# Cross attention's first keys and values are made in the self stage, with the output projection, norm and queries in waves of chunks behind it

## What is computed

```python
x = x + gate * (self_attention(norm(x)) @ w_so + b_so)      # keys: the batch's 256 tokens
q = norm(x) * scale + shift @ w_q                           # "cq"
k, v = ctx @ w_k + b_k, ctx @ w_v                           # "ck", "cv", 1601 keys
x = x + gate * (softmax(q k / sqrt(8)) v @ w_co + b)        # layer 2: only the 16 largest scores
x = x + gate * mlp(norm(x))
```

## Time and profile before

| | |
|---|---|
| median of 3 runs | 4952.71 us (4948.7 to 4954.18) |
| profiled execution | 4945.83 us, its span 4944.1 us |
| granted TensorE clock, mean | 0.798 of full |
| busy share | PE 70%, DVE 73%, ACT 58%, POOL 11% |
| six attention stages begin at | 188, 398, 1193, 1406, 2249 and 2476 us |

### The profile page before, as it was taken

How to read it: one execution, slowest core, us unless ns; L and a number is a source line. 1 busy time by engine, 2 the same in 40 slices (tenths; PEclk the granted TensorE clock), 3 DMA queues, 4 the chain that set the end, 5 groups by cost and what they waited for, 6 DMA issues and landing times. The chain is left out here.

```text
span 4944.1 us, 75874 instructions
## 1 busy us (share of the span) xinstructions
PE 3477.9 (70%) x28020; PEld 1517.5 (31%) x28020; DVE 3632.0 (73%) x5577; ACT 2860.3 (58%) x5351; POOL 556.4 (11%) x1277
## 2 busy tenths in 40 slices
PE   2575999975759999865636656565666665578987
PEld 2222333322223333332213223232322222235553
DVE  6555888935567888735479999999999999923223
ACT  1353888853517887834437777777777776622123
POOL 1011212100114334001100100000010100000000
PEclk7776999986769999976657777767776777689999
DMA  4424434204343343115231101110110100001000
GB/s 129 115 53 104 98 88 102 62 20 106 66 102 87 75 94 82 33 49 100 60 68 37 36 23 32 31 38 22 34 39 21 33 13 13 2 21 34 20 0 9
DMA packets 270142, 265.81 MB, mean 54 GB/s; under 512 B 48976, under 2 KB 238808, under 8 KB 269016
## 3 DMA queue, kind: packets, MB, share of 16 engines
q1 hardware_dynamic: 269784, 261.10, 22.1%
HBM read 150.71 MB, written 109.09 MB: 53 GB/s over the span
## 5 line engine op out<-in xcount | busy, mean ns | idle before, releaser
L1096 ACT ACTIVATE prob<-x_ps 128x512 f32<-128x512 f32 (+1 forms) x2880 | 1563.5, 597 | 426.0 <-PE x_ps L994 401.9
L1187 DVE TENSOR_REDUCE mpart<-ring 128x1 f32<-128x400 f32 (+2 forms) x2816 | 1292.7, 523 | 325.2 <-PE ring L942 321.9
L942 PE MATMUL ring<-k_st,q_st 52*128 52x400 bf16 (+2 forms) x3584 | 860.8, 372 | 436.3 <-ACT s_sb L1078 320.4
L1013 PE MATMUL av_ps<-prob,va 128*16 128x256 f32 (+1 forms) x11520 | 990.0, 433 | 2.3 <-ACT o_sb L1102 1.8
L994 PE MATMUL x_ps<-q_st,k_st 55*128 55x256 bf16 x5504 | 625.1, 302 | 78.4 <-ACT prob L1096 48.7
L989 PE MATMUL x_ps<-neg_id,un 128*128 128x128 bf16 (+1 forms) x3328 | 364.1, 276 | 364.0 <-ACT prob L1096 362.4
L1069 ACT ACTIVATE un<-s_sb 128x1601 fp8e4<-128x1601 f32 x256 | 392.7, 1535 | 352.0 <-DVE s_sb L1213 352.0
L942 PEld LDWEIGHTS ring<-k_st,q_st 52*128 52x128 bf16 x3584 | 256.1, 101 | 952.6 <-ACT s_sb L1078 400.4
L1078 ACT ACTIVATE s_sb<-ring 128x400 f32<-128x400 f32 (+1 forms) x1024 | 472.0, 525 | 43.7 <-PE ring L942 35.5
L1202 DVE MAX8 mpart<-s_sb 128x8 f32<-128x1601 f32 x256 | 455.2, 1826 | 20.0 <-ACT s_sb L1078 20.0
L1206 DVE MATCH_REPLACE8 s_sb<-mpart,s_sb 128x1601 f32<-128x1601 f32 x256 | 463.2, 1824 | 0.0
(11 more groups left out here) (194 smaller groups left out, 3294.5 us busy)
## 6 DMA issues: line engine op xcount, KB each, us to landing
k_st<-kc_dram SPq DMA_DIRECT2D x192, 300.2 KB, 5.3
kc_dram<-k SPq DMA_DIRECT2D x432, 100.0 KB, 2.3
q_dram<-pj_q SPq DMA_DIRECT2D x144, 128.0 KB, 2.3
q_st<-q_dram SPq DMA_DIRECT2D x80, 192.0 KB, 3.8
kc_dram<-k SPq DMA_DIRECT2D x144, 100.2 KB, 2.3
ctx_t<-in_ctxT SPq DMA_DIRECT2D x16, 800.5 KB, 5.1
o_dram<-o_sb SPq DMA_DIRECT2D x768, 9.0 KB
k_dram<-pj_q SPq DMA_DIRECT2D x72, 128.0 KB, 2.3
```

The source lines that it names most:

```text
L942: nc.tensor.matmul(ring_ps[:, r % BANKS, 0:w], q_st[rows, b % NQ, 2 * t + pl, qt * P:(qt + 1) * P], k_st[rows, slot_of(n), pl, c0:c0 + w], ...
L1013: last = nc.tensor.matmul(av_ps[32 * k:32 * k + VW, n % 2, :], va[0:sizes[j], b % NVB, j, G * t + k, :], prob[0:sizes[j], s % NPROB, (2 * ...
L1096: nc.scalar.activation(prob[0:size, s % NPROB, hf * 512:(hf + 1) * 512], x_ps[0:size, (2 * s + hf) % XBANKS, :], ACT.Exp, scale=HEAD_SCALE ...
L1187: nc.vector.tensor_reduce(mpart[:, n % 4, row, c:c + 1], ring_ps[:, r % BANKS, 0:chunks[c][1]], AX.X, ALU.max).then_inc(g["red"].sem, 1)
```

## The change

`stage_project(cross)` is gone. What it did is a class `Onward`, called at the end of the self stage; the keys and values of batch 0 are items of the self stage's plan. The order of the waves: chunk c begins at wave FIRST[c], and in each wave every begun chunk does its next step.

```diff
+Q_AHEAD = 2
...
+        self.va = self.sb("va", [P, 2, CT, NH, VW])
...
+            nc.gpsimd.memset(p.va[:], 1.0).then_inc(loaded.sem, 1)
...
+class Onward:
+    FIRST = (0, 1, 2, 5)
+    OP, MEAN, VAR, DIAG, NORM, PROJ = range(6)
...
+    def waves(self, first, upto):
+        for w in range(first, upto):
+            for c in range(NC):
+                k = w - self.FIRST[c]
+                if 0 <= k < 6:
+                    yield k, c
...
+    def pe(self, pe, ready, exps, ocopy):
...
+            if k == self.OP:
+                pe.wait_ge(ready.sem, ready.at(2 * c + 2))
...
+                nc.tensor.matmul(self.bank[:, c, :], weight(p, self.layer, "so"), p.o_all[:, cols], start=True, stop=True).then_inc(s["op"].sem, 1)
...
+            elif k == self.MEAN:
...
+                pe.wait_ge(s["x"].sem, s["x"].at(c + 1))
...
+    def pool(self, pool, table):
+        done = 0
+        for c in (1, 2):
+            done = self.split(pool, self.p.nc.gpsimd, self.s["pchain"], done, c, self.s["pparts"], table)
...
+    def sp(self, sp, x_done, stores):
+        p, s = self.p, self.s
+        k_st = p.k_flat[:].rearrange("p (t h c) -> p t h c", t=NG, h=2)
+        sp.wait_ge(x_done.sem, x_done.at(2 * NU * 2))
+        for st in stores:
+            sp.wait_ge(st.sem, st.at(192))
+        for t in range(NG):
+            for hf in range(2):
+                sp.dma_start(k_st[64 * hf:64 * hf + STACK, t], p.kc_dram[0, 2 * t:2 * t + 2, hf].rearrange("h r c -> r h c")).then_inc(s["loaded"].sem, 16)
+        for c in range(NC):
+            parts = s["dparts" if c in (0, 3) else "pparts"]
+            sp.wait_ge(parts.sem, parts.at(1 + c // 2))
+            for j in range(GROUPS):
+                sp.dma_start(p.q_dram[:, :, j * HD:(j + 1) * HD, c * CH:(c + 1) * CH].rearrange("h f d c -> (h f) d c"), self.q3[:, c, Q_PART[j]]).then_inc(s["st" if c else "st0"].sem, 16)
+            if c == 0:
+                sp.wait_ge(s["st0"].sem, s["st0"].at(16 * GROUPS))
+                for b in range(Q_AHEAD):
+                    for hf in range(2):
+                        sp.dma_start(p.q_st[64 * hf:64 * hf + STACK, b], p.q_dram[:, hf, :, b * T:(b + 1) * T].rearrange("h r c -> r h c")).then_inc(s["loaded"].sem, 16)
...
+            for b in range(1, B) if cross else [0]:
...
+        if not self.cross:
+            return (4 if self.KU == 8 else 8) * (i + 1)
...
+        if not self.cross:
+            return 36 + 4 * i
...
+            load_ctx(B0)
...
-                for b, c in kstore_at[-1]:
-                    store_k(b, c)
-                for n in kload_at[-1]:
-                    load_k(n)
-                load_ctx(1)
...
+            if onward:
+                onward.sp(sp, g["x"], [g["kst0"], g["kst1"]])
...
-                nc.vector.memset(va[:], 1.0).then_inc(g["init"].sem, 1)
...
+                if onward and k == END + 2:
+                    onward.dve_begin(dve)
+                    onward.dve(dve, 0, 2, table)
                 for b in recip_at.get(k, []):
                     recip(b)
+                if onward and k == END + 6:
+                    onward.dve(dve, 2, 3, table)
+            if onward:
+                if rope:
+                    dve.wait_ge(g["tab"].sem, g["tab"].at(16))
+                onward.dve(dve, 3, onward.ALL, table)
```

More of the change, by code:

```diff
@@ L484, in stage_project @@
             table = p.sb("pj_table", [P, 2, T], F32, ctx)
[L485 to L486 removed]
+        va = p.sb("pj_va", [P, NV, 4, NH, VW], F32, ctx)
         pp = p.ps("pj_ps", [P, 3, CH], ctx)
[L488 removed]
         block = ctx.enter_context(nc.Block())
@@ L525, in _ @@
                     nc.tensor.matmul(pp[:, n % 3, :], weight(p, layer, names[r]), norm.h[:, c, :], start=True, stop=True).then_inc(proj.sem, 1)
[L526 to L535, removed]
+            for g in range(NV):
+                m = NI * stepn + g
+                if g < 3:
+                    pe.wait_ge(pf.sem, pf.at(m - 2))
+                else:
+                    pe.wait_ge(v_out.sem, v_out.at(g - 2))
+                for k in range(4):
+                    last = nc.tensor.matmul(pp[:, m % 3, k * P:(k + 1) * P], norm.h[:, g, k * P:(k + 1) * P], weight(p, layer, "v"), start=True, stop=True)
+                last.then_inc(v_mm.sem, 1)
         @block.scalar
@@ L547, in _ @@
                 ins.then_inc(pf.sem, 1)
[L548 to L558, removed]
+            act.wait_ge(ones_r.sem, ones_r.at(1))
+            for g in range(NV):
+                m = NI * stepn + g
+                act.wait_ge(v_mm.sem, v_mm.at(g + 1))
+                nc.scalar.activation(va[:, g, :, :, 0:HD], pp[:, m % 3, :].rearrange("p (k h d) -> p k h d", k=4, d=HD), ACT.Copy).then_inc(v_out.sem, 1)
+        @block.gpsimd
+        def _(pool):
+            nc.gpsimd.memset(va[:], 1.0).then_inc(ones_r.sem, 1)
         @block.vector
         def _(dve):
-            if cross:
-                out.dve(dve)
             norm.dve(dve)
@@ L584, in _ @@
                 done += 3
[L585 to L591, removed]
+    v_mm.passed(NV)
+    v_out.passed(NV)
+    v_st.passed(32 * NV)
+    ones_r.passed(1)
     if rope:
@@ L678, in stage_attention @@
     masked = layer == 2 and not cross
-    rope = layer == 1 and cross
+    rope = layer == 1
     biased = layer != 1
@@ L687, in stage_attention @@
     KSTEP = 2 if rope else 1
-    KU, VU = (4 * KSTEP, 4) if cross else (0, 0)
+    KU, VU = 4 * KSTEP, 4
+    B0 = 1 if cross else 0
+    ahead = range(1, B) if cross else [0]
+    q_index = lambda b: b // NQ + (1 if not cross or b % NQ >= Q_AHEAD else 0)
     BANKS, XBANKS = 4, 3
```

318 lines of the change are left out of this document (227 added, 91 removed).

## The result

The changed kernel took 4841.28 us (median of 3, 4840.75 to 4842.8) against 4952.71: a ratio of 0.9785, 95% interval 0.9772 to 0.9798. The forecast was 4866, a ratio of 0.9825, 25 us too slow; the result lies inside the stated range (4822 to 4908), but 6 us under the forecast's own range (4847 to 4884). The profiled execution took 4842.8 us with a span of 4841.0, so 103.1 us of span against the earlier trace rows.

The account below looks back on a forecast made before the run. No single engine bounds the whole; SP's queue is full in the self stage. 139 - 46 - 2 - 4 = 87 us saved from 4952.7 gives 4866 us, range 4822 to 4908.

Parts of the forecast that it names:

- The waves, 139 us: Last value matmul to cross stage's first score: 139 us saved over three layers, between 121 (low clock) and 158 (high).
- The late normalise: End of self stage: DVE's first waves delay the last normalise by 10 us at low clock, 5.8 at high.
- The prediction's 111: Cross stages' start: batch 0's keys and values no longer made there, first score earlier, 111 us gained over three layers.
- The key stores, 46 us on SP: Self stages: four groups of six key stores on SP's full queue cost 15.4 us per layer, 46 in all.
- absorbed: Rival: SP's key stores in the self stage cost almost nothing; 133 us saved, 4820 us; chance 0.12.
- slower at 1.8 us a store: Rival: SP's key stores issue slowly in the self stage; kernel slower from 1.8 us each, 4978 at 2.16; chance 0.04.
- The engines' part, costed at nothing: Self stages: PE's and ACT's added work for keys and values costs nothing; up to 29 us if not covered.
- The table of layer 1 (2 us): Start of self stage: layer 1's 1.6 MB table load delays the first row loads, 2 us taken between 0 and 10.
- GpSimd beside DVE, 4 us: Waves: two of chunk 3's DVE steps slowed by GpSimd beside them, 0.7 us each, 4 us for three layers.
- The signs of being wrong: Self stage grows under 8 or over 25 us; first score waits beyond zero matmul; GpSimd's chunk 2 ends the stage.
- Waves without use: Rival: waves at the self stage's end hide nothing; 30 us saved, 4923 us; chance 0.12.
- Engines without cover: Rival: new matmuls and copies between scores stall the self stage, all 29 us of PE's added; 4895 us; chance 0.12.

Follow-up runs that it names:

- e12: The changed kernel as it is, measured once more on the same chip as three other runs: ratio 0.9792 to the kernel before.
- e3: The changed kernel with only key tile 0 loaded at the self stage's end, tiles 1 to 3 at the cross stage's start: ratio 0.9793.
- e7: Half the change: batch 0's keys and values in the self stage, projection in its own stage, key loads waited for at that stage's end: ratio 0.9896.
- e9: The changed kernel with one store for each six key stores and twelve key loads of eight rows instead of eight loads: ratio 0.9850.
- e10: The changed kernel with one store for six, twelve eight-row key loads, and half of chunk 3's query stores on ACT's queue: ratio 0.9843.
- e5: The changed kernel with two long-row stores for each six key stores in the self stage, so scores read misplaced keys: ratio 0.9727.
- e1: The changed kernel with each group of six key stores in the self stage issued twice: ratio 0.9893.
- e6: The changed kernel with each self-stage matmul that makes batch 0's keys and values issued twice into the same bank: ratio 0.9805.
- e11: The changed kernel with the four chunks one after another instead of in waves: ratio 0.9958.
- e2: The changed kernel with the self stage's key stores issued by ACT's queue instead of SP's, at the same steps: ratio 0.9763.

## Why the prediction was right, point by point

**The waves, 139 us.** Measured 138.9 (40.5, 51.4 and 47.0 by layer), in e12 140.2. The forecast took the middle between the low clock (121) and the high one (158; its figures by layer add up to 120 and 157); the clock was 0.79 to 0.88 up to the last normalise and 0.61 to 0.67 behind it. That the middle fits so well is partly luck. SP's wait behind the key loads (2.9 us in layer 0, 0.9 in layer 2, against the 6.1 of e3) was not in the layout, and its premise, that the self stage's tail runs at the low clock, held in one layer of three. The late normalise was 6.0, 4.5 and 6.4 us later, near the high clock's 5.8 and not the low one's 10; batch 6's reciprocal came 7.0 us after the last value matmul, not 10. Chunk 3 ends the stage and not GpSimd's chunk 2, ready at 381.8, as forecast. Keys alone are worth 91 of the 139 (e7). The prediction's 111 for them shrinks by 20 where the projection keeps a stage of its own: the query loads then stand ahead of the first score, 3.5 us a layer, and the three layers together take 10 us longer from last value to next stage.

**The key stores, 46 us on SP.** The self stage up to its last row load grew by 51.5 us (mean of seven executions). The four store counts, 12, 24, 72 and 144 for the three layers, give 440.2 (e9, e10), 449.9, 474.8 and 528.6 us. From 12 to 72 a store costs 0.58 us; the line reaches 433 at none, so the stores' part is 42 us, against a forecast of 46. (The stores of e5 and e9 are fewer and larger, but take as long to issue, 0.59 us.) The step was right in mechanism and size, and the rivals "absorbed" and "slower at 1.8 us a store" are both refuted by e1. The time alone would not have told: 4841 lies 25 us from the forecast and 21 from "absorbed" (4820). The experiments separate the two, and what brought the result so near to that rival is the term that the sum missed, below.

**The engines' part, costed at nothing.** This term was most likely too small. At no stores 433 us are left where the kernel before had 423.3: some 10 us for the new matmuls, copies, splits and the context load together, but from a line drawn past its points and against a single profile. e6 points the same way: 25 us of the same matmuls once more cost 6 to 8 us. "SP's queue, always full, is what they can be waiting for" was then too strong: idle time of 25 of 105 us did not make all of it free. Why is not shown; that they sit between scores in the ring is the likely reason, and the copies and GpSimd's splits were never tried alone. The table of layer 1 (2 us) cannot be told from this.

**GpSimd beside DVE, 4 us.** The diagonal on DVE took 0.93 to 1.62 us in four of its twelve instances, each time just behind the start of a GpSimd operation (three times of chunk 2's split, once of the last normalise), instead of 0.63 to 0.69. For chunk 3's, the ones that I had priced, that is 0.6, 0.2 and 0.9 us more in layers 0 to 2; its residual, the other one, never met GpSimd and kept its 0.69. So 1.8 us stand against the 4 forecast, and they are inside the 138.9 measured, where I had counted them on top. Layers 0 and 1 of the changed kernel, both engines in order of time:

```profile
359.45 0.63 DVE L764 TENSOR_TENSOR on_f<-const,on_rstd 128x512 f32<-128x512 f32 x1
359.48 1.18 POOL L1348 TENSOR_TENSOR o_all<-num,rden 128x256 f32<-128x256 f32 x1 [5.37 <-DMA rden<-r_dram]
...
363.50 0.72 POOL L1348 TENSOR_TENSOR o_all<-num,rden 128x256 f32<-128x256 f32 x1 [2.84 <-DMA rden<-r_dram]
363.55 1.22 DVE L764 TENSOR_TENSOR on_f<-const,on_rstd 128x512 f32<-128x512 f32 x1
...
1354.81 1.27 POOL L714 TENSOR_TENSOR on_f<-on_f,table 128x512 f32<-128x512 f32 x1 [15.54 <-ACT on_h L705]
1355.35 0.69 DVE L769 TENSOR_TENSOR on_h<-on_h,xa_ps 128x512 f32<-128x512 f32 x1 [4.59 <-PE xa_ps L668]
...
1360.44 0.61 POOL L724 CAST on_q<-on_f 128x512 bf16<-128x512 f32 x1
1360.67 0.93 DVE L764 TENSOR_TENSOR on_f<-const,on_rstd 128x512 f32<-128x512 f32 x1 [0.27 <-ACT on_rstd L686]
```

The product with its operand in PSUM (`xa_ps`) keeps its 0.69 us beside GpSimd's, the diagonal with both in SBUF does not. All four slow diagonals end 0.55 us after the GpSimd operation that had begun before them, as if they had stood still until it was over; at 359.45 the diagonal began first, kept its 0.63, and GpSimd's product took 1.18 instead of 0.72. The rule of the Trainium skill that the forecast weighed (SBUF — State Buffer, "Who interferes with whom") says the same, and the 20 us of the other reading did not come.

**The sum, 87 us, was 16 us too small** by the first pair of profiles (103.1). The terms above account for little of it: 4 more from the last point, 4 from the stores, 2 from the table, 10 less for the engines, and 4 more because this profile's 470.9 lies that much under the mean. Together that is 4 of the 16. The rest, less 2 us lost elsewhere in the program, is a term I did not have, the stretch from last row load to last value matmul: 43.5 us in all before, 30.0 after, so 13.5. It was left out of the sum, and how large it comes out is a matter of the execution: in e12 it is 5.8, and from self stages to first scores 93.8 us are saved where the forecast says 87. Over the seven executions of the same code the stretches sum to 26 to 40 us, mean 34.5, which is 9 less than in the one profile of before. That the change causes it is not shown: it follows the clock, below. By medians the gain was 111 us in the first measurement. The profile of before lies 6.9 us under its median and that of after 1.5 over, and what no row explains of the 111 is in that.

**The signs of being wrong.** One of them came up. "It is wrong if the self stage grows by under 8 us or over 25 in a layer": up to the last value matmul layer 0 grew by 7.8 us, layers 1 and 2 by 12.6 and 13.6. Up to the last row load, where SP's stores act, it was 15.2, 16.5 and 15.9, as forecast; in layer 0 the last stretch then ran at 1.00 and took 8.1 us, where it had taken 15.5 at 0.50. In e12 layer 0 grew by 16.3. It was a poor sign, since the level of the clock in one short stretch moves this quantity by 4 to 6 us. The other two did not come up: the first score waits for the zero matmul alone, and chunk 3 ends the stage. From the last normalise to the first score it is 34.6, 42.0 and 32.0 us, within the 26 to 46 given.

**The rivals.** "Waves without use" fell to the change's own trace and to e7: the waves take 47.7 us off the separate stage. e11 shows what the merged projection costs with no waves, 0.9958 or some 4932 us, close to that rival's 4923. "Engines without cover" (29 us) fell to e6, though some 10 us of it seem to have come true.

## What to carry to other kernels

A queue that issues DMAs back to back is a bound that no busy share shows: count the issues and take the median of the same instruction. For the first 24 stores per layer that came out within a tenth (42 us for 46), for the next 24 a seventh too low (46 for 54). When work moves into a stage bounded so, do not cost the engines' part at nothing; the best reading here is that a quarter to a third of PE's part was felt. An order that delays an operation on the longest chain can still pay, if what runs in its place would otherwise run behind that chain: lay out both orders before moving it.

## What was not expected of the hardware

**Loads of few rows.** Twelve loads of eight partitions (200 KB each) moved at 80 GB/s with a DMA share of 0.54, eight loads of 48 partitions at 166 GB/s with 0.95. The packets are the same in both (768 of 3202 bytes for the keys, and the same query stores). Issues behind them were slow too: six query stores took 14.7 us to issue instead of 3.8. Half the rate at about half the share is what would be seen if such a load ran on only half of the 16 DMA engines; the trace does not tell the engines apart, so this is not shown.

**The clock in the last 8 to 15 us of a self stage.** In the 39 such stretches of the thirteen changed kernels' profiles the granted clock was either 1.00 (15 times, 7.9 to 9.4 us) or 0.50 to 0.52 (24 times, 12.0 to 15.2 us), for 77 to 107 matmuls: the two levels of 2.4 and 1.2 GHz. In layer 0 it was high in the first profile of the change, low in e12. In the first profile PE was busy for 5.89 of 8.1 us in layer 0 and for 10.15 of 12.8 us in layer 2, on 85 and 87 matmuls. The kernel before had the low level in all three. More than one self stage in three is thus 4 to 6 us shorter than its twin. Over the seven executions of the same code the three stretches together differ by up to 14 us, so a single pair of profiles can show 10 us that a change has not made.

**The cost of an issue on ACT.** A group of six stores on ACT's queue took ACT about as long as SP (3.7 us for five) and left ACT idle for 3.41 us ahead of its next exponential, though ACT was busy for only 69 of 105 us in that stage (e2).
